# A graph layer pair on one core: products of t and h alternate in two rounds per strip instead of seven

## The reference, cut to what matters

```python
def reference(x, adj, W_u, diag_u, par_u, W_i, diag_i, par_i, gamma, beta, W1, b1):
    # x 5120x64, adj 5120x5120, both f32
    u = par_u[0] * par_u[1] * (diag_u[:, None] * x[:2048] @ W_u) + x[:2048]
    i = par_i[0] * par_i[1] * (diag_i[:, None] * x[2048:] @ W_i) + x[2048:]
    e = concatenate([u, i])
    h = adj @ (adj.T @ e)                       # t = adj.T @ e, then h = adj @ t
    x = layernorm(x + layernorm(h) * gamma + beta + x)
    deg = adj.sum(axis=0) + 1
    dinv = rsqrt(deg)
    z = dinv[:, None] * (x @ W1)
    g = relu(dinv[:, None] * (adj.T @ z + z) + b1)
    return layernorm(x + g)
```

## Time and profile before

| | us |
|---|---|
| median of 3 runs | 670.77 |
| lowest, highest | 670.51, 672.86 |
| the profiled execution, its own time | 669.55 |
| its span, first to last instruction | 667.8 |
| first pass, strips pipelined (59.2 to 401.3 in the trace) | 342.1 |
| one strip in the middle of it | 37.8 |

### The profile page before, as it was taken

One profiled execution on the slowest core, in us unless ns is written; L12 is line 12 of the kernel. 1 busy time (PEld: TensorE's weight loads), 2 busy tenths in 40 slices (PEclk: granted clock), 3 DMA queues, 4 the chain that ended last, 5 costly groups with the idle time before them and its releaser, 6 DMA issues.

```text
span 667.8 us, 15832 instructions
## 1 busy us (share of the span) xinstructions
PE 607.5 (91%) x7290; PEld 279.2 (42%) x7290; DVE 319.3 (48%) x357; ACT 138.5 (21%) x208; POOL 106.8 (16%) x126
## 2 busy tenths in 40 slices
PE   2498999999999999999999999999999999778772
PEld 1343444544545454544545457554343333112111
DVE  1177585877858585866848486231040404004004
ACT  0201524060604214060603215411000101001001
POOL 2080404040402204040402204010000000000000
PEclk9999999999999999999999999999999999999997
DMA  8948769869595979969595923999999999999990
GB/s 246 356 154 302 252 233 341 292 236 330 201 341 199 340 251 313 320 213 335 209 327 200 360 67 130 386 399 408 409 409 413 408 413 409 413 410 409 414 362 16
DMA packets 92197, 204.10 MB, mean 306 GB/s; under 512 B 14780, under 2 KB 14820, under 8 KB 92132
## 3 DMA queue, kind: packets, MB, share of 16 engines
q1 hardware_dynamic: 80724, 200.31, 80.2%
q10 hardware_dynamic: 11408, 2.79, 1.9%
HBM read 201.78 MB, written 1.31 MB: 304 GB/s over the span
## 4 chain that ended last, share of the span: by engine, by line
PE 77%; DMA 14%; ACTq 3%; DVE 3%; ACT 1%; issue 1%; DVEq 0%
PE psum L723 32%; PE psum L815 22%; DMA slot<-in_adj_dram 11%; PE psum L905 11%; PE psum L823 5%; DMA turned<-in_adj_dram 3%; PE psum L717 2%; PE psum L764 2%; ACTq L370 2%; DVE cut L571 1%; ACTq L355 1%; PE psum L777 1%; PE psum L887 1%; PE psum L915 1%; PE psum L876 1%; PE psum L791 1%
## 5 line engine op out<-in xcount | busy, mean ns | idle before, releaser
L571 DVE STREAM_TRANSPOSE cut<-slot 128x2048 f32<-128x2048 f32 x80 | 177.8, 2281 | 79.4 <-PE psum L815 79.1
L723 PE MATMUL psum<-slot,E 128*64 128x512 f32 x872 | 202.8, 599 | 0.0
L815 PE MATMUL psum<-cut,T 32*64 32x256 f32 x5120 | 155.2, 379 | 2.4 <-ACT T L389 1.3
L815 PEld LDWEIGHTS psum<-cut,T 32*64 32x64 f32 x5120 | 111.0, 131 | 69.5 <-issue 46.0
L341 POOL COPY turned<-cut_last 32x1024 f32<-32x1024 f32 x80 | 82.9, 1036 | 279.4 <-PE psum L823 252.3
L723 PEld LDWEIGHTS psum<-slot,E 128*64 128x64 f32 x872 | 57.4, 136 | 113.3 <-issue 113.3
L398 ACT ACTIVATE turned<-cut_last 32x1024 f32<-32x1024 f32 x80 | 84.4, 1055 | 15.3 <-DVE cut_last L571 8.3
L905 PE MATMUL psum<-slot,E 128*64 128x512 f32 x288 | 68.7, 598 | 9.9 <-DMA slot<-in_adj_dram 9.9
L389 ACT ACTIVATE T<-T 32x256 f32<-32x256 f32 x60 | 24.8, 414 | 249.8 <-DVE T L549 248.6
L665 DVE TENSOR_TENSOR T<-psum,E 128x256 f32<-128x256 f32 x10 | 4.2, 425 | 147.0 <-PE psum L915 146.5
L905 PE MATMUL psum<-cut,E 128*64 128x512 f32 x224 | 53.5, 598 | 7.0 <-DMA cut<-in_adj_dram 7.0
(11 more groups left out here) (110 smaller groups left out, 270.1 us busy)
## 6 DMA issues: line engine op xcount, KB each, us to landing
slot<-in_adj_dram SPq DMA_DIRECT2D x136, 1024.0 KB, 8.1
cut<-in_adj_dram SPq DMA_DIRECT2D x35, 1024.0 KB, 18.3
cut_last<-in_adj_dram SPq DMA_DIRECT2D x10, 1024.0 KB, 15.9
turned<-in_adj_dram SPq DMA_DIRECT2D x10, 1024.0 KB, 18.3
X<-in_x_dram ACTq DMA_DIRECT2D x5, 256.0 KB, 13.3
out_dram<-T ACTq DMA_DIRECT2D x10, 128.0 KB, 9.7
T<-in_L_gnn_W_u_dram ACTq DMA_DIRECT2D x2, 16.0 KB, 2.8
T<-in_L_gnn_W_i_dram ACTq DMA_DIRECT2D x2, 16.0 KB, 7.4
```

The costliest lines, as they stand in the source:

```text
L571: v.transpose(to.rearrange("p c (j k r) -> p j k c r", j=JB, r=Q32), slot[c % NS][:, :, :].rearrange("p k (j c r) -> p j k c r", j=JB, r=Q ...
L723: return mm(acc[half[b % 2], :], E[:, b, :], view[:, b % CB, :], start=(b < 2), stop=(b >= NB - 2))
L815: last = mm(acc[half[h], a, u * 2 * P:(u + 1) * 2 * P], T[step % 2][rows_a, jb, (c - a) % 4, :], cut[u][rows_a, c, h, :, jb * P:(jb + 1) * P],
```

## The change

T_GROUPS = 7 becomes T_ROUNDS = 2. In `h_step`, in place of seven pieces of t between eight h groups, there are two rounds: ten pairs of t (chunks 0 to 4 of the next strip), four h groups (unit 0), ten pairs of t (chunks 5 to 9), four h groups (unit 1). The same matmuls are made with the same operands; semaphore signals stay on the same instructions. In the last strip, which has no t to come, the order is as before.

```diff
-T_GROUPS = 7
+T_ROUNDS = 2
...
                 final = step == NJ - 1
-                for n in range(UNITS * JB):
-                    u, jb = n // JB, n % JB
-                    if not final and n < T_GROUPS:
-                        t_pairs(step + 1, n * HS // T_GROUPS, (n + 1) * HS // T_GROUPS)
+                for n in range(T_ROUNDS):
+                    u, jb = n * UNITS // T_ROUNDS, n * UNITS * JB // T_ROUNDS % JB
+                    if not final:
+                        t_pairs(step + 1, n * HS // T_ROUNDS, (n + 1) * HS // T_ROUNDS)
                     if n == 0:
                         pe.wait_ge(t_ready, step * 2 + 2)
                         pe.wait_ge(spread_act, (step + 1) * len(ACT_COPIES))
                         pe.wait_ge(spread_dve, (step + 1) * len(DVE_COPIES))
                     if jb == 0:
                         pe.wait_ge(chunk_cut, cuts_of(step, range(u * UQ, (u + 1) * UQ)))
-                    last = h_group(step, u, jb)
-                    if jb == JB - 1:
+                    for i in range(UNITS * JB // T_ROUNDS):
+                        last = h_group(step, u, jb + i)
+                    if jb + i == JB - 1:
                         last.then_inc(unit_used if not final else h_done, 1)
```

## The result

The changed kernel takes 722.95 us (median of 4 runs, 719.53 to 726.49), the kernel before 671.82 (4 runs, 670.51 to 673.80): a ratio of 1.076, 95% interval 1.069 to 1.083. It is slower, as forecast, but by 51 us and not by 17; the time lies far outside the range of 678 to 697.

The account below looks back on a forecast made before the run. PE bounds the first pass; switches save 1.7 us a steady strip, waits cost 4.1. Eight such strips add 20.0, the first takes off 2.6: 669.55 + 17.4 = 687.0, in medians 688.2, stated as 688.5; range 678 to 697.

Parts of the forecast that it names:

- What bounds the kernel: First pass: bound by PE and nothing else, busy 37.80 of 37.80 us in one strip's window.
- the price of a switch: Between t and h: 0.34 us a pair; five pairs less save 1.7 us a strip, 15.3 over nine strips.
- The waits for chunks 3 and 4: First round of t in a steady strip: PE waits 1.3 and 1.9 us, 3.35 lost in all.
- Chunk 9: Second round of t in a steady strip: its load lands at 26.75 us, so PE waits 0.75.
- The late cuts: DVE's four cuts that release loads: start at −0.96 us and stay tied to turn_t, whether PE is earlier or later.
- S: Start of a strip's first product of t, 174.38 in the profiled strip; the prediction's times are distances from it.
- Four h groups of unit 0: 4 × 1.727 + 0.19 = 7.1: Unit 0's run of h behind the first round: takes 7.1 us, ending at 19.1 in a steady strip.
- The first strip: h_step(0): chunks 3 and 4 in time, so the strip ends at 36.9 us against 39.56, −2.6.
- The waits slow PE's clock: Rival: each steady strip pays a slowed clock once on its longest wait, +14, 702 us; chance 0.04.
- DVE's copy: Before turn_t: the copy is done at 33.3 us, 2.4 to spare before 35.75, so turn_t isn't delayed.

Follow-up runs that it names:

- four rounds: Four rounds per strip, each five pairs of t and two column blocks of h, against the kernel before: 661.82 us, ratio 0.986.
- The kernel with short runs: Changed kernel's loop with four rounds of 10, 2, 6 and 2 pairs of t, two column blocks of h behind each: 692.50 us, ratio 1.028.
- the kernel with waits of 4 to 6 us: Changed kernel's loop with ten pairs of t first, then the other ten in twos between single h groups: 752.41 us, ratio 1.118.
- the kernel of three rounds: Three rounds of six, seven and seven pairs of t with three, three and two column blocks of h: 678.96 us, ratio 1.012.
- the quarter loads: Changed kernel with first-pass loads from the third strip on cut to one of four row blocks: 658.20 us, ratio 0.981; order of before likewise cut: 673.71 us.
- the kernel of six and fourteen: Two rounds as in the changed kernel, but six pairs of t in the first and fourteen in the second: 681.99 us, ratio 1.016.

## Why the prediction went wrong

- **What bounds the kernel, and the price of a switch: right.** 0.34 us a pair is confirmed twice, by 36.79 with four rounds and 36.12 with two and a quarter of the loads.
- **The waits for chunks 3 and 4: right, a little large.** Forecast 3.35 us in the first round, measured 11.35 − 8.68 = 2.7, since chunk 4 landed at +9.3 to +9.9 rather than +10.1 (at +8.5 in one strip). Chunk 9: forecast 0.75 idle, measured 0.5 to 0.8 in seven of eight steady strips. The late cuts kept their distance to S, as argued, in all steady strips but h_step(7), whose S came late: PE had ended the strip before at the fallen clock. The kernel with short runs shows this cause alone.
- **The failed step is "Four h groups of unit 0: 4 × 1.727 + 0.19 = 7.1", and the same 7.1 for unit 1.** Measured 9.80 and 8.48, 4.1 us a strip or 33 of the 50 us, the fallen clock included: PE ran out of instructions where a block ended inside the run. The rate of 1.727 comes from groups that had t close by the earlier trace rows, and from the last strip, where 256 records ran through the earlier trace rows; there the transfer of the block that they needed had begun at 409.46, before the next loads of adj were issued (from 410.35 on). I took a rate that PE reached under one supply of instructions for its rate under any, and no rival had this wait.
- **The first strip: wrong by 2.1.** 39.01, not 36.9: unit 1's run broke off there too (8.63 in place of 7.1), and the second round took 10.04 in place of 9.55, with a wait of 1.08 us for chunk 9 where 0.7 was forecast.
- **The rival "The waits slow PE's clock": in part.** It was given 0.04, at 14 us. The clock did fall, in 2 of 8 steady strips, and cost about 5 us, but behind the idle stretches in h and not behind the waits that the rival named; the kernel with waits of 4 to 6 us lost it in every strip. Most idle stretches of 1.3 to 2.0 us didn't do it, one of 1.29 did.
- **DVE's copy:** its cover of 2.4 us held, and showed its worth in the kernel of three rounds, which used it up.

What stays open: why a transfer of instructions often begins 3 us late when loads are in flight. That the loads have a part in it is shown by the quarter loads; whether the delay is in the request, in a queue or in an engine is not. In the kernel of six and fourteen the transfers that began over 2 us behind PE's entry into a block of h had four or five loads issued and not landed, all but the first, and those that began under 2 us had one or two while loads went on; but in the changed kernel two to four were enough, so their number isn't the whole of it. Nor can the trace tell when PE's sequencer asks for a block, only when PE enters the one ahead: some transfers began up to 5.6 us before that.

## What to carry to other kernels

A long run of short matmuls beside heavy loads can eat instructions faster than they are brought, as here. Count the instructions in the run, and if 256 of them last less than a transfer's delay and length together (here 3.45 us against 3 + 2.45), put long ones in between. An interleaving that looks like overhead, seven switches at 0.34 us, may be what hides loads, instruction blocks and another engine's chain; thin it out until the first of these shows, and not further: here four rounds, 661.8 us, ratio 0.986. A measured rate belongs to its surroundings.

## What the runs showed of the hardware

- PE's instructions come in transfers of 16,384 bytes, 256 instructions of 64 bytes; PE went on 2.3 to 2.6 us behind the start of the transfer that it had waited for.
- Such a transfer often begins later when loads are in flight: mostly 2 to 3.6 us behind PE's entry into the block ahead where PE ran dry, against at most 1.7 inside h with a quarter of the traffic. It isn't always so: 0.5 and 1.0 us in two unbroken runs at 386 and 385 GB/s.
- The granted clock fell to half behind three of the idle stretches of 1.3 to 2.2 us (0.96 and 0.93 in two windows), behind four of 1.6 to 1.9 us in the kernel of six and fourteen pairs, and in each steady strip with a wait of 4 to 6 us.
